# A router product with the high and low weights side by side, in the feed-forward stage of a transformer layer

## What is computed

```
x = x + layernorm(attention(layernorm(x)))
x = x + layernorm(ffn(layernorm(x)))

def ffn(x):                                   # H = 256, I = 176, E = 8, K = 2
    probs = softmax(x @ Wr)                   # Wr: 256 x 8, the router
    w, idx = top_k(probs, 2); w = w / sum(w)
    combine = sum_k(w_k * onehot(idx_k))      # one row of 8 per token
    y_e = (silu(x @ Wg[e]) * (x @ Wu[e])) @ Wd[e]    # for all 8 experts
    return sum_e(combine[e] * y_e)
```

## Time and profile before

| what | value |
|---|---|
| timed runs, median of 3 | 2121.91 us (2121.78 to 2122.18) |
| profiled execution, its own time | 2123.74 us |
| its span, first to last instruction | 2122.0 us |
| TensorE busy, share of the span | 97% |
| mean granted TensorE clock | 0.985 |

### The profile page before, as it was taken

One profiled execution on the slowest core, in us unless ns is written; L12 is line 12 of the kernel. 1 busy time (PEld: TensorE's weight loads), 2 busy tenths in 40 slices (PEclk: granted clock), 3 DMA queues, 4 the chain that ended last, 5 costly groups with the idle time before them and its releaser, 6 DMA issues.

```text
span 2122.0 us, 36773 instructions
## 1 busy us (share of the span) xinstructions
PE 2055.5 (97%) x13268; PEld 1871.5 (88%) x13268; DVE 1729.2 (81%) x2519; ACT 1411.4 (67%) x2575; POOL 1548.7 (73%) x1329
## 2 busy tenths in 40 slices
PE   6999999999999999999999999999999999849998
PEld 5899999989999999999999999899989999848887
DVE  7889878887989888988898888878888889865553
ACT  5777666776777767776777677767776777624333
POOL 2779777886878777876797788877797778845333
PEclk9999999999999999999999999999999999969999
DMA  4667667766667666765777576766676667720000
GB/s 105 156 156 179 154 143 163 165 162 160 147 159 174 153 147 157 176 159 136 164 174 164 132 164 161 178 146 153 154 174 142 148 147 166 193 72 1 11 11 21
DMA packets 216598, 298.50 MB, mean 141 GB/s; under 512 B 44896, under 2 KB 85344, under 8 KB 216416
## 3 DMA queue, kind: packets, MB, share of 16 engines
q1 hardware_dynamic: 216416, 296.15, 59.5%
HBM read 25.46 MB, written 2.10 MB: 13 GB/s over the span
## 4 chain that ended last, share of the span: by engine, by line
PE 85%; DVE 4%; SPq 4%; POOL 3%; ACT 2%; DMA 1%; issue 1%; POOLq 0%; DVEq 0%; ACTq 0%
PE ps_s L497 15%; PE ps_s L498 15%; PE ps_s L499 14%; PE ps_a L499 13%; PE ps_a L498 13%; PE ps_a L497 13%; SPq L316 3%; POOL pT_lo L409 3%; ACT probs L815 1%; PE ps_a L745 1%; PE ps_a L748 1%; PE ps_a L747 1%; DVE part_max L1061 1%; DMA pT<-probs 1%; PE ps_s L731 0%
## 5 line engine op out<-in xcount | busy, mean ns | idle before, releaser
L409 POOL TENSOR_TENSOR pT_lo<-pT,pT_hi 128x512 fp32r<-128x512 f32 x1024 | 1302.8, 1302 | 361.0 <-ACT pT_hi L828 359.7
L828 ACT ACTIVATE pT_hi<-pT 128x512 fp32r<-128x512 f32 x1024 | 613.0, 628 | 226.6 <-DMA pT<-probs 157.6
L815 ACT ACTIVATE probs<-ps_s,shift 128x1024 f32<-128x1024 f32 x512 | 566.6, 1109 | 226.0 <-DVE shift L1070 225.9
L1061 DVE TENSOR_REDUCE part_max<-ps_s 128x1 f32<-128x1024 f32 x512 | 622.0, 1217 | 68.5 <-PE ps_s L499 67.0
L1080 DVE STREAM_TRANSPOSE probs<-probs 128x1024 f32<-128x1024 f32 x512 | 619.4, 1229 | 64.7 <-ACT probs L815 63.7
L497 PE MATMUL ps_a<-pT_hi,v_hi 128*128 128x256 f32 x2048 | 578.8, 283 | 1.7 <-POOL pT_lo L409 1.6
L499 PE MATMUL ps_a<-pT_hi,v_lo 128*128 128x256 f32 x2048 | 580.0, 283 | 0.0
L498 PE MATMUL ps_a<-pT_lo,v_hi 128*128 128x256 f32 x2048 | 579.8, 283 | 0.0
L497 PE MATMUL ps_s<-kT_hi,qT_hi 128*128 128x512 f32 x1024 | 405.0, 395 | 11.7 <-ACT probs L815 8.6
L497 PEld LDWEIGHTS ps_a<-pT_hi,v_hi 128*128 128x128 f32 x2048 | 392.0, 191 | 19.7 <-POOL pT_lo L409 2.9
L498 PEld LDWEIGHTS ps_a<-pT_lo,v_hi 128*128 128x128 f32 x2048 | 392.0, 191 | 15.5
(11 more groups left out here) (161 smaller groups left out, 2935.8 us busy)
## 6 DMA issues: line engine op xcount, KB each, us to landing
pT<-probs SPq DMA_DIRECT2D x2048, 128.0 KB, 2.5
pT<-in_L_attn_x SPq DMA_DIRECT2D x4, 512.0 KB, 5.5
codes<-in_L_attn_wk_codes SPq DMA_DIRECT2D x16, 128.0 KB, 2.4
scales<-in_L_attn_wk_scales SPq DMA_DIRECT2D x64, 32.0 KB, 3.0
codes<-in_L_attn_wo_codes SPq DMA_DIRECT2D x16, 128.0 KB, 2.3
scales<-in_L_attn_wo_scales SPq DMA_DIRECT2D x64, 32.0 KB, 1.8
x<-in_L_attn_x SPq DMA_DIRECT2D x4, 512.0 KB, 7.5
layer_out<-x SPq DMA_DIRECT2D x8, 256.0 KB, 2.1
```

The lines of the kernel that those rows point to most:

```text
L409: pool.tensor_tensor(pT_lo[:, p, :].rearrange("p (i n) -> p i n", i=Q4), pT[:, s % 2, g, :, t:t + 2, :].rearrange("p i t q -> p i (t q)"), ...
L815: nc.scalar.activation(out, src, ACT.Exp, bias=shift[:, s % SLOTS, r:r + 1], scale=SCALE, accum_out=sums[:, s % SLOTS, r, g:g + 1])\
L828: nc.scalar.activation(pT_hi[:, p, :].rearrange("p (i n) -> p i n", i=Q4), pT[:, s % 2, g, :, t:t + 2, :].rearrange("p i t q -> p i (t q)" ...
L1061: V.tensor_reduce(part_max[:, s % SLOTS, r, g:g + 1], ring_of("s", w, NG2 * r + g), AX.X, ALU.max)\
```

## The change

The high and low parts of the router's weights lie side by side in one tile, `wr_both`: per half of the features, 8 columns of high and 8 of low. One matmul of `xT_hi` with all 16 columns makes high x high and high x low in 16 PSUM columns, and one of `xT_lo` with the 8 high columns adds low x high to the first 8. So a row tile has four matmuls in place of six, and the two parts of a logit lie 8 columns apart in PSUM. VectorE sums them in a new reduction into the new tile `logits` in SBUF, waits for it by the new semaphore `logits_summed`, and takes the maximum and the subtraction from there.

```diff
-        wr_hi = sb("wr_hi", [P, DC, E], f32r)
-        wr_lo = sb("wr_lo", [P, DC, E], f32r)
+        wr_both = sb("wr_both", [P, DC, 2, E], f32r)
...
+        logits = sb("logits", [P, TPC, E], f32)
...
-            pool.tensor_copy(wr_hi[:, :, :], wr_raw[:, :, :]).then_inc(sm["wr_hi_done"], 1)
+            pool.tensor_copy(wr_both[:, :, 0, :], wr_raw[:, :, :]).then_inc(sm["wr_hi_done"], 1)
             pool.wait_ge(sm["wr_hi_done"], 1)
-            pool.tensor_tensor(wr_lo[:, :, :], wr_raw[:, :, :], full(wr_hi[:, :, :]), ALU.subtract)\
+            pool.tensor_tensor(wr_both[:, :, 1, :], wr_raw[:, :, :], full(wr_both[:, :, 0, :]), ALU.subtract)\
                 .then_inc(sm["wr_lo_done"], 1)
...
                     for a in range(TPC):
                         rows = slice((TPC * c + a) * P, (TPC * c + a + 1) * P)
                         for cc in range(DC):
-                            last = product3(ps_pre[:, a * E:(a + 1) * E], xT_hi[:, cc, rows], xT_lo[:, cc, rows],
-                                            wr_hi[:, cc, :], wr_lo[:, cc, :], first=cc == 0, last=cc == DC - 1)
+                            nc.tensor.matmul(ps_pre[:, 2 * a * E:2 * (a + 1) * E], xT_hi[:, cc, rows],
+                                             wr_both[:, cc, :, :].rearrange("p h e -> p (h e)"),
+                                             start=cc == 0, stop=False, skip_group_check=True)
+                            last = nc.tensor.matmul(ps_pre[:, 2 * a * E:(2 * a + 1) * E], xT_lo[:, cc, rows],
+                                                    wr_both[:, cc, 0, :], start=False, stop=cc == DC - 1,
+                                                    skip_group_check=True)
                     last.then_inc(sm["logits_ready"], 1)
...
                     dve.wait_ge(sm["logits_ready"], c + 1)
-                    logits = ps_pre[:, 0:TPC * E].rearrange("p (t e) -> p t e", e=E)
-                    V.tensor_reduce(lmax[:, :], logits, AX.X, ALU.max).then_inc(sm["lmax_done"], 1)
+                    parts = ps_pre[:, 0:2 * TPC * E].rearrange("p (t h e) -> p t e h", e=E, h=2)
+                    V.tensor_reduce(logits[:, :, :], parts, AX.X, ALU.add).then_inc(sm["logits_summed"], 1)
+                    dve.wait_ge(sm["logits_summed"], c + 1)
+                    V.tensor_reduce(lmax[:, :], logits[:, :, :], AX.X, ALU.max).then_inc(sm["lmax_done"], 1)
                     dve.wait_ge(sm["lmax_done"], c + 1)
-                    V.tensor_tensor(ex[:, :, :], logits, lmax[:, :].unsqueeze(2).to_broadcast([P, TPC, E]),
+                    V.tensor_tensor(ex[:, :, :], logits[:, :, :], lmax[:, :].unsqueeze(2).to_broadcast([P, TPC, E]),
                                     ALU.subtract).then_inc(sm["lsub_done"], 1)
```

More of the change, by code:

```diff
@@ L167, in sandwich_layer @@
             stat1 aggr1 eps1 std1 rstd1 z_norm x1_done stat2 aggr2 eps2 std2 rstd2 xn2_done xn2_t xT2_hi xT2_lo
-            logits_ready lmax_done lsub_done ex_done gt_done ge_done ties_done beats_done rank_done sel_done
+            logits_ready logits_summed lmax_done lsub_done ex_done gt_done ge_done ties_done beats_done rank_done sel_done
             wsum_done winv_done comb_ready comb_t combT_hi combT_lo
```

## The result

| | before | changed |
|---|---|---|
| timed runs, median | 2122.18 us (7 runs, 2118.13 to 2124.11) | 2115.05 us (7 runs, 2111.57 to 2119.64) |
| profiled execution, its own time | 2123.74 us | 2117.04 us |
| span | 2122.0 us | 2115.3 us |

The ratio of the times is 0.9965 with a 95% interval of 0.9954 to 0.9975: faster by 7.4 us, between 5.3 and 9.8. The forecast was 2113.4 us in a range of 2111.7 to 2117.0, 8.5 us less than before.

The account below looks back on a forecast made before the run. TensorE was taken to bound the feed-forward stage, with a slack-free chain in chunk 0. Gains of 0.73 (chunk 0), 2.68 (chunks 1 to 3) and 5.1 (clock falls) sum to 8.5 us: 2113.4 us, range 2111.7 to 2117.0.

Parts of the forecast that it names:

- Which engine bounds, and chunk 0's chain: Feed-forward stage: TensorE bounds after 1896 us; chunk 0's slack-free chain gets 1.71 - 0.25 = 1.46 us shorter.
- Chunks 1 to 3, 2.68 us: Routers of chunks 1 to 3: 8 fewer matmuls each at 0.112 us save 2.68 us; VectorE's new sum costs nothing.
- The clock's return: After chunk 0: return to full clock stays at its moment, so 0.73 of 1.46 us is kept.
- The falls, 5.1 us: Routers of chunks 2 and 3: half-clock stretches of 3.4 and 6.8 us both vanish with shorter routers, saving 5.1 us.
- rival B: Clock falls: one is left, or timed runs have one fewer to lose; 2115.1 to 2116.8 us, chance 0.10.
- The sum: Whole kernel: 0.73 + 2.68 + 5.1 = 8.5 us gain, median 2121.91 to 2113.4 us.
- A, both falls stay: Chunks 2 and 3: clock falls remain, only matmul count helps; 3.4 us gain, say 2118.2 us, chance 0.13.
- C, accumulation that waits for itself: Router matmuls of unlike width on one PSUM region wait for each other; 9.7 us slower, 2131.6 us, chance 0.03.
- D: Nothing comes of the change because another engine takes over; 2121.9 us, chance 0.02.

Follow-up runs that it names:

- second group of runs: Changed kernel timed again as reference against the kernel before on the same chip: 2117.27 us (6 runs) against 2125.50 (23 runs), ratio 0.9958.
- second profile: Kernel before, no edit, profiled again: 236.9 us from first router matmul to end of span; half clock for 6.8, 3.4, 3.4 us in chunks 1, 2, 3.
- 30 extra matmuls: Changed kernel plus unread 512-column matmuls (12, 3, 3, 12) in the gaps of chunk 0's preparation: 2112.89 us, ratio to before 0.9943.
- with 42: Changed kernel plus unread 512-column matmuls (14, 6, 6, 16) in the gaps of chunk 0's preparation: 2111.57 us, ratio to before 0.9950.

## Why the prediction was right, step by step

**Which engine bounds, and chunk 0's chain.** Right. The chain shrank by 1.45 us of the 1.46 forecast, made of 8 intervals of 0.213 us less one reduction of 0.225 us and its hand-over.

**Chunks 1 to 3, 2.68 us.** The interval at 16 columns is 0.111 us, the value taken. Nothing of it was lost to VectorE: the sum is hidden, and the wait for `comb` in chunk 1 is unchanged.

**The clock's return.** Forecast was that it would not move with the work, so that only 0.73 of 1.46 us are kept. Measured from the first router matmul, the clock returned after 12.7, 13.2 and 11.8 us in the profiles before and after 12.9, 12.9 and 11.6 us in those after: 0.1 us apart on average, while the work behind it starts 1.44 us earlier. The half-clock part of that work grew from 3.3 to 4.7 us, which costs 0.7. The return comes at times that differ between executions of one kernel by over a microsecond, so three profiles each show this only as an average. The Trainium skill, "TensorE: Matmul & The Clock Gate", Part 1, says that the monitor behind the clock isn't reset when a kernel starts; the traces agree in so far as the return came anywhere from 2.6 to 5.2 us behind the transposes of `comb`.

**The falls, 5.1 us.** The largest term, argued then, and now shown: at equal count and pace, streaming 256 columns instead of 8 in a third of the matmuls removes the falls and 5.7 us. The ground given, that a router of 1.8 us is shorter than what had run before either fall, held in chunks 1 to 3: in all profiles the falls there began 2.1 to 4.8 us behind the first router matmul. It is no safe limit, as the last section shows. Its size was read from one profile, and there luck helped: half of the time at half clock is 5.1, 6.8 and 5.1 us in the three profiles, 5.7 on average. From the second one the same working would have given 0.73 + 2.68 + 6.8 = 10.2 us, above the 5.3 to 9.8 measured. The doubt that the timed runs might have fewer falls than the profile (part of rival B) found no support: each of three profiles had two or three, and in the second group of runs the mean granted clock was 0.9853 over 23 timed runs before and 0.9875 over 6 of the changed kernel. One side argument was idle: that half of the matmuls are twice as wide plays no part, since 16 matmuls of 8 columns keep the clock up too.

**The sum.** 0.73 + 2.68 + 5.1 = 8.5 us forecast. By stage over three profiles each, 8.8 measured; the terms, with half of the time at half clock taken as lost, give 1.44 - 0.7 + 2.68 + 5.7 = 9.1. The difference lies in the falls. Set against the changed kernel from router to router, and less 0.89 us of matmuls per chunk, they cost 5.0, 5.8 and 5.0 us, 5.3 on average; ahead of chunk 1's router 0.8 us are saved (44.0 us from chunk 0's for 44.8), and 0.8 + 2.68 + 5.3 = 8.8. The second profile's fall of 6.8 us in chunk 1 cost 2.4 us and not 3.4: from chunk 1's router to chunk 2's it took 56.33 us, where the other two, with no fall there, took 53.92. They have TensorE's wait of 0.57 us for `comb` there, and it has not: the one wait listed for TensorE in that profile from 1925 to 2100 us is another (total us, times, longest us).

```profile
PE ps_s L686 <- DVE acc L998: 0.4, 1, 0.4
```

Timed, the gain is 7.4 us (5.3 to 9.8) in the first group of runs and 8.9 (0.0042 x 2125.5; 6.0 to 11.9) in the second. The absolute forecast was 1.65 us too low, which the scatter of both kernels' runs, 6 and 8 us wide, covers.

**The rivals.** A, both falls stay, fell: none stayed, in three profiles. B, one fall is left, fell with it. The rule of the Trainium skill that spoke for A ("TensorE: Matmul & The Clock Gate", "Why this matters for your kernels", no long idle gap between bursts of matmuls) doesn't cover this kernel: the clock falls here with TensorE busy 4.00 us of 4.00, so that its being without a gap was not enough. C, accumulation that waits for itself, fell with the 0.111 us interval. D fell with the stage.

## What to carry to other kernels

A stretch of back-to-back matmuls that stream few columns costs twice: once by count, since 8, 16 and 256 columns cost nearly the same interval here (0.111, 0.111 and 0.12 us), and again by the clock, which fell to half for 3.4 or 6.8 us, most of it dense work behind the stretch. Look at the granted clock by stretch, not at the mean (0.985 before, 0.986 after), and put narrow products side by side; where they can't be made fewer, wide matmuls among them kept the clock up here. Compare a short stage by its own duration in several profiles when the rest of the kernel scatters by more than the gain.

## What the runs showed of the hardware that was not expected

- **Attention scatters.** In profiles of kernels whose attention is the same, the first router matmul starts anywhere from 1884.3 to 1890.6 us. The timed medians of the kernel before were 2122.18, 2123.05 and 2125.50 us in three groups of runs. Three first runs within 0.4 us of each other gave no hint of that. Where the scatter arises was not looked into.
- **A fall can follow 16 narrow matmuls.** With 30 extra matmuls the clock fell for 3.4 us at the end of chunk 0's router, 2.0 us behind its first matmul, where the work before it had had gaps (busy 2.48 of 4.00 us), and no longer did with 42 (3.85 of 4.00).
- **32 narrow matmuls in a row can pass without one**, as chunk 1 shows in the kernel with 8 more than before. What decides a single case stays open.
